# Relative attention: the skewed reads of a unit issued on GpSimd's queue instead of SyncE's

## The reference

```python
dist = jnp.clip(idx[None, :] - idx[:, None], -R, R) + R
pe_k = rel_emb_k[dist]
pe_v = rel_emb_v[dist]
score = jnp.einsum('bhqd,bhkd->bhqk', q, k) + jnp.einsum('bhqd,qkd->bhqk', q, pe_k)
attn = jax.nn.softmax(score, axis=-1)
ctx = jnp.einsum('bhqk,bhkd->bhqd', attn, v) + jnp.einsum('bhqk,qkd->bhqd', attn, pe_v)
```

## Time and profile before

| | |
|---|---|
| median of 3 runs | 1867.73 us (1867.34 to 1868.03) |
| the profiled execution | 1865.14 us, its span 1863.3 us |
| relative attention, first to last skewed transfer | 651 to 1037 us of the span |
| PE busy over the span | 87% |
| DVE / ACT / POOL busy | 65% / 36% / 15% |

### The profile page before, as it was taken

The page is one execution under the profiler, slowest core; times in us unless marked ns, Lnnn a source line. Parts: engine busy times, 40 slices in busy tenths (PEclk is TensorE's granted clock), DMA queues, the critical chain, the costliest instruction groups (busy, mean ns, idle before and its releaser), DMA issues. The chain is left out here.

```text
span 1863.3 us, 38531 instructions
## 1 busy us (share of the span) xinstructions
PE 1627.8 (87%) x14742; PEld 1280.3 (69%) x14742; DVE 1207.3 (65%) x3881; ACT 675.0 (36%) x1408; POOL 271.8 (15%) x240
## 2 busy tenths in 40 slices
PE   6799987889988679888888689498899999999998
PEld 4677765656656556777776467377688788878876
DVE  3555653455556546566666339528889889888894
ACT  3333331255555246566666143013222222222210
POOL 1443444100000100000000004301001000100000
PEclk9899998999999878999999775599999999999999
DMA  3100000001011379899998430341000000000000
GB/s 123 46 18 18 18 24 6 18 19 36 14 58 47 100 280 319 312 319 315 332 331 306 134 84 23 137 177 56 2 2 13 13 2 13 13 2 13 2 7 13
DMA packets 96469, 175.32 MB, mean 94 GB/s; under 512 B 16032, under 2 KB 80800, under 8 KB 91552
## 3 DMA queue, kind: packets, MB, share of 16 engines
q1 hardware_dynamic: 96288, 172.85, 26.7%
HBM read 93.01 MB, written 79.69 MB: 93 GB/s over the span
## 5 line engine op out<-in xcount | busy, mean ns | idle before, releaser
L104 PE MATMUL bank<-per_xT,per_down 128*128 128x256 f32 x1024 | 252.1, 392 | 2.3 <-ACT per_xT L2400 1.6
L2703 PE MATMUL bank<-per_up,per_act_w 128*128 128x256 f32 x1024 | 242.1, 382 | 0.0
L2703 PEld LDWEIGHTS bank<-per_up,per_act_w 128*128 128x128 f32 x1024 | 195.2, 191 | 26.9
L104 PEld LDWEIGHTS bank<-per_xT,per_down 128*128 128x128 f32 x1024 | 191.3, 193 | 30.2 <-issue 2.7
L2407 ACT ACTIVATE per_act_w<-bank 128x512 f32<-128x512 f32 x128 | 76.2, 597 | 363.9 <-PE bank L104 329.3
L1508 ACT ACTIVATE rel_probs<-rel_summed,rel_low 128x256 f32<-128x256 f32 x256 | 117.3, 519 | 26.8 <-DVE rel_low L1592 26.7
L1592 DVE CUSTOM_DVE_ANT_0 rel_summed<-bank,rel_bias 128x256 f32<-128x256 f32 x256 | 94.9, 419 | 36.5 <-PE bank L1706 21.3
L920 DVE TENSOR_REDUCE xat_mx<-bank 128x2 f32<-128x512 f32 x128 | 79.4, 683 | 32.7 <-PE bank L968 32.6
L104 PE MATMUL bank<-ret_x2T,ret_w_in 128*128 128x256 f32 x384 | 93.1, 399 | 7.5 <-issue 7.5
L2386 POOL TENSOR_TENSOR per_sim<-per_sim,per_best_i 128x512 f32<-128x512 f32 x32 | 41.8, 1328 | 333.9 <-DVE per_sim L2520 333.9
L1727 PE MATMUL bank<-rel_band_k,rel_qT 32*128 32x191 f32 x512 | 63.2, 370 | 31.1 <-DVE rel_low L1592 23.7
(11 more groups left out here) (354 smaller groups left out, 3191.3 us busy)
## 6 DMA issues: line engine op xcount, KB each, us to landing
rel_qr_rows<-rel_qr SPq DMA_DIRECT2D x32, 1024.0 KB, 8.0
rel_p_rows<-rel_probs SPq DMA_DIRECT2D x32, 1024.0 KB, 6.6
rel_bias<-rel_qr_rows SPq DMA_DIRECT2D x64, 384.0 KB, 4.4
rel_by_dist<-rel_p_rows SPq DMA_DIRECT2D x64, 384.0 KB, 4.7
per_down<-in_per_down SPq DMA_DIRECT2D x1, 4096.0 KB, 25.2
per_up<-in_per_up SPq DMA_DIRECT2D x1, 4096.0 KB, 12.4
ret_xin<-in_x SPq DMA_DIRECT2D x8, 256.0 KB, 2.9
xat_cT<-in_contextT SPq DMA_DIRECT2D x8, 256.0 KB, 3.0
```

The lines of the kernel that those rows point to most:

```text
L104: last = pe.matmul(dst, wt[:, c], src[:, c, :], start=c == 0, stop=c == DC - 1)
L2703: last = pe.matmul(tiles(bank[7])[:, t, :], act_w[:, n % 2, k, t * P:t * P + P], up[:, k, :], start=k == 0, stop=k == COLS - 1)
```

## The change

The two blocks that issue the skewed reads move from SP's list to POOL's, to the head of the step, and their order is exchanged: the bias reads of unit s+2 come first, the dist reads of unit s second. Their waits, sources and targets are as before. POOL's own two operations now stand behind them in the step.

```diff
             for s in STEPS:
-                if (U := turn_of(s)) is not None:
-
-                    sp.wait_ge(p_saved[U % 2], 16 * (U // 2 + 1))
-                    if U >= 3:
-                        sp.wait_ge(wT_mm, 2 * (U - 2))
-                    for t, first in ((0, 2 * NEAR), (1, 0)):
-                        skewed = bass.AP(p_rows[U % 2].tensor, first, [[2 * PW + 2, P], [PW, 2], [1, 2 * NEAR]])
-                        sp.dma_start(by_dist[:, U % 3, t, :, 0:NEAR].rearrange("p h k e -> p h (k e)"), skewed)\
-                            .then_inc(dist_loaded[U % 3], 16)
-                if (U := unit(s + 2)) is not None:
-
-                    sp.wait_ge(qr_saved[U % 2], 16 * (U // 2 + 1))
-                    ...
                 if (b := out_of(s - 1)) is not None:
                     sp.wait_ge(y_ready, b + 1)
 ...
             for s in STEPS:
+                if (U := unit(s + 2)) is not None:
+
+                    pool.wait_ge(qr_saved[U % 2], 16 * (U // 2 + 1))
+                    if U >= 2:
+                        pool.wait_ge(summed_ready, 4 * (U - 1))
+                    for t, first in ((0, 2 * (P - 1)), (1, 2 * (2 * P + REACH - 2))):
+                        ...
+                        pool.dma_start(bias[:, U % 2, t, :, REACH * t:REACH * t + NEAR]
+                                     .rearrange("p h k e -> p h (k e)"), skewed).then_inc(bias_loaded[U % 2], 16)
+                if (U := turn_of(s)) is not None:
+
+                    pool.wait_ge(p_saved[U % 2], 16 * (U // 2 + 1))
+                    ...
                 if (b := x_turn_of(s - 1)) is not None:
                     pool.wait_ge(turned, b + 1)
```

More of the change, by code:

```diff
@@ L1489, in _ @@
             for s in STEPS:
+                if (U := unit(s + 2)) is not None:
[3 more added lines that the diff above has]
+                    for t, first in ((0, 2 * (P - 1)), (1, 2 * (2 * P + REACH - 2))):
+                        skewed = bass.AP(qr_rows[U % 2].tensor, first, [[2 * PW - 2, P], [PW, 2], [1, 2 * NEAR]])
+                        pool.dma_start(bias[:, U % 2, t, :, REACH * t:REACH * t + NEAR]
+                                     .rearrange("p h k e -> p h (k e)"), skewed).then_inc(bias_loaded[U % 2], 16)
+                if (U := turn_of(s)) is not None:
+                    pool.wait_ge(p_saved[U % 2], 16 * (U // 2 + 1))
+                    if U >= 3:
+                        pool.wait_ge(wT_mm, 2 * (U - 2))
+                    for t, first in ((0, 2 * NEAR), (1, 0)):
+                        skewed = bass.AP(p_rows[U % 2].tensor, first, [[2 * PW + 2, P], [PW, 2], [1, 2 * NEAR]])
+                        pool.dma_start(by_dist[:, U % 3, t, :, 0:NEAR].rearrange("p h k e -> p h (k e)"), skewed)\
+                            .then_inc(dist_loaded[U % 3], 16)
                 if (b := x_turn_of(s - 1)) is not None:
```

## The result

The change made the kernel slower: 1912.19 us as a median (1912.03 to 1913.6), against 1867.88 before on the same chip, a ratio of 1.0236 [1.0218, 1.0253], or 44 us. The forecast was 1887 with a range to 1918: right in direction, and the time lies in the range, but the loss is more than twice the 19 us that the sum gave. The profiled execution took 1912.28 us (span 1910.5), 47 more than that of before.

The account below looks back on a forecast made before the run. PE and the engines feeding it were taken to set the pace, transfers just keeping up. Terms 8.8 + 2.4 + 1.1 + 5.0 + 1.5 = 18.8 us on 1865.1 gave 1884, stated as a median of 1887, range 1866 to 1918.

Parts of the forecast that it names:

- What bounds the kernel: In the layer, PE and its feeding engines set the pace; transfers just keep up, DMA engines 91% busy.
- SP loses four issues: SP's queue: dropping the reads frees 2.3 us a step, moves writes at most 1 us; put at 0.
- Exchanging bias and dist: Dist reads some 3.2 us later, hidden except at the layer's end; bias reads gain 0.3 us.
- The price c of a read on POOL: POOL's time to issue one read: taken as 1.0 us, bounded by 0.44 and 1.86.
- Term A: Out steps: the power stands behind four reads, so normalise is 2.39 us late; five steps cost 8.8 us.
- Terms B and C: Layer's end: late normalise and last dist reads, 2.4 us; layer's start: first bias reads waited for, 1.1 us.
- Terms D and E: Six steps where the bias is last, 0.8 us each, 5.0; steps where it is just in time, 1.5 together.
- Costly reads: Rival: POOL's reads cost 1.6 us or more each, perhaps as DVE holds POOL up; 1910 to 1930; 1.5 in 10.
- As cheap as SP: Rival: a read costs POOL at or below 0.5 us, time stays at 1866 to 1870; 1.5 in 10.
- Faster by sharing: Rival: two queues share the DMA engines, so bias reads land earlier; 1857 with landing 2 us less; 1 in 10.
- What I said would disprove me: Changed profile: L141 never waits for POOL, qr write's landing changes by over 1 us, or DVE's copies grow longer.

Follow-up runs that it names:

- experiment 2: Changed kernel with the old order of the reads on POOL (dist first, bias second): 1903.57 us, 1.02.
- experiment 6: Kernel before with all reads on SP in the old order, the p and qr writes issued by ACT: 1899.59 us, 1.0158.
- experiment 1: Kernel before, all on SP, with only the reads' order exchanged (bias first, then dist): 1926.59 us, 1.0319.
- experiment 9: Changed kernel with the qr write ahead of the p write on SP; reads stay on POOL, bias first: 1869.03 us, 0.9993.
- experiment 3: Changed kernel with POOL's power at the head of its step, ahead of the reads: 1911.61 us, 1.0244.
- experiment 10: Qr write and bias reads first up to step 26, old orders behind: kernel before so edited, 1862.77 us; changed kernel, also power first, 1879.37 us.
- experiment 5: Changed kernel, p write held until bias reads are issued: 1926.24 us; also dist and power first: 1898.58; dist first, held until bias reads land: 1913.8.
- the last run of experiment 4: Kernel before with only the dist reads moved to POOL and the power at the head of POOL's step: 1884.26 us, 1.0089.

## Why the prediction was right or wrong

**What bounds the kernel.** Right: PE sets the pace, the transfers just keep up, and any lateness of the bias reads is paid. The conclusion from 91% busy DMA engines was incomplete: that share holds only because of an order that keeps them fed. Left out altogether was that PE's own work may take longer: 25.5 of the layer's 45.6 us are longer busy time for the same matmuls, at a clock of 0.87 instead of 0.93.

**SP loses four issues: put at 0. This step failed.** I counted SP's time of issue, and asked which write would go earlier, but not what that write would then do to the reads. SP's list also kept each pair of bias reads ahead of the next p and qr writes (901.44, 902.40, 903.02). Without it, with the order of the reads as before, the loss is 34 us (experiment 2), the larger part of the 44; with ACT as the second queue it is 31 us, ACT's own part included (experiment 6).

**Exchanging bias and dist: put at hidden, with a gain of 0.3 us a step. This step failed, and most clearly.** Alone it costs 57 us (experiment 1). I saw that the dist reads go 3.2 us later and asked only whether their consumer could wait. The question was what the DMA engines move in the meantime: in experiment 1, for some 3 us of each step, little or nothing. The cost is paid mostly by the next bias reads (59.8 us of waits in `add_bias`, 6.2 in `far_sums`). In the changed kernel the exchange adds only some 10 us to the second queue's 34, but turning the writes round to match it gives back all 44 (experiment 9).

**The price c of a read on POOL.** 1.0 taken, 0.73 measured; the sum by its own bound for 0.71 was 6.5 us. The right direction came from a price that was too high. The 44 us come from elsewhere. A right sign with the time inside the stated range was luck.

**Term A, 8.8 us.** The mechanism was there, smaller (L141 waits 7.5 us in seven times instead of 1.6 in two), and worth nothing measurable once the bias reads are late (experiment 3).

**Terms B and C, 2.4 and 1.1 us.** The wait of `far_sums` at the end is 2.4 us against 2.2, so the dist reads' longer issue hardly shows. The start is not separated from the rest by a run.

**Terms D and E, 5.0 and 1.5 us.** The place was right: the steps in which the bias reads come last or just in time. The size was not: a late step loses 3 to 7 us, not 0.8, since the reads are issued nearer to the scores and move beside up to 2.75 MB of other traffic, instead of standing 1.1 us further back. The count was short by one step as well: before, at 998.37, `add_bias` starts 2.49 us after the scores though its row names PE. The idle time of `add_bias` grew by 35 us where D and E had 6.5.

**The rivals.** Costly reads: no; the issue of a bias read takes 0.72 us at the least and at the median and 0.96 at the most, which leaves little room for DVE holding POOL up. The Trainium skill ("SBUF — State Buffer", section "Who interferes with whom") says that DVE in its 2-port modes blocks GpSimd for a whole instruction; no instruction at a doubled rate was seen in the earlier trace rows, and no such delay either, which agrees. As cheap as SP: near to it in c, and still wrong in time. The Trainium skill's rule behind it ("DMA: Bandwidth & Descriptors", section "Issuing engines are not separate DMA queues"), that another issuing engine only saves time of issue, gave the right time in experiment 9, where POOL issues all reads at no loss, and the wrong one in experiments 2, 6 and 10. It says nothing of the order between two lists. Faster by sharing: the qr write did gain (8.0 to 6.9 us), but the reads paid for it, the opposite of the condition. The sentence against that rival, that sharing "shifts time to the qr write, the one before the bias", had the sign of the share wrong.

**What I said would disprove me** came true in one point: the qr write's landing moved by 1.1 us, "sharing of the DMA engines matters more than issue".

**Open.** How the DMA engines divide their time between two queues, packet by packet, no row shows; only the landing times do. How much of experiment 2's 34 us is sharing and how much a changed rhythm of the writes is not settled: the holds (experiment 5) remove the one and bring the other. The power first holds back the reads behind it while POOL waits for the variance (792.24 against 790.46 in experiment 10, and all five out steps of the last run of experiment 4); how this grows to 7 us one step later is open. And whether the granted clock falls because PE waits is not shown, only that both go together.

## What to carry to other kernels

When reads follow writes through DRAM, issue the reads in the order of their writes, so that one pair moves while the other write is being confirmed; when one order is exchanged, exchange the other with it. On two queues that isn't enough: put the pair first whose reads are waited for (experiment 9 against 2). Before moving transfers to another queue, write down which later transfers they stand ahead of on the old one: that order is lost, and no semaphore says so. When transfers are late while the DMA share falls, look at single microseconds of a step: a share of 0.00 between two bursts says that no queue had anything to move. And count PE's busy time for the same matmuls: what looks like waiting can be paid for a second time in the granted clock.

## What the runs showed of the hardware that I had not expected

- A read of 256 rows of 1.5 KB costs GpSimd 0.73 us of issue, beside 0.44 us on SyncE. Its queue moves 50.34 MB in 14336 packets, 3.5 KB each, more than the row of 1.5 KB.
- A second queue, served by GpSimd or by ACT, slows the median read by at most 0.8 us (4.4 us to 5.2 and 4.6) and its tail by more (6.3 to 9.8 and 11.0). A long landing is no loss by itself: in experiment 9 a read of 9.0 us costs 0.7, since it was issued 8 us ahead of the scores.
- A list order alone, with the same transfers and engines, is worth 57 us of 1868.
- The same 2861 matmuls keep PE busy 317.0 us at a mean granted clock of 0.93, 342.5 at 0.87 and 344.2 at 0.86 (one of them missing in the last two traces).
